# Attention and gated feed-forward on one core: one PSUM bank for queries and keys, one for values and transposed input, two buffers behind them

## What is computed

```python
x = x + layernorm(attention(layernorm(x), W_Q, b_Q, W_K, b_K, W_V, b_V, W_O, b_O))
x = x + layernorm(ffn(layernorm(x), weight, gate_w, lora_U, lora_V))

# attention, 16 heads of 64:
Q, K, V = x W_Q + b_Q, x W_K + b_K, x W_V + b_V
attn = softmax(Q K^T / sqrt(64));  out = (attn V) W_O + b_O
# ffn, 8 experts of rank 16:
gate = softmax(x gate_w^T)
out = x weight^T + sum_e gate_e * (x U_e^T) V_e^T / 16
```

## Time and profile before

| | |
|---|---|
| median of 3 runs | 1090.09 us |
| profiled execution | 1091.16 us |
| its span, first to last instruction | 1089.3 us |
| PE busy | 1021.8 us (94%) |
| DVE busy | 905.9 us (83%) |
| ACT busy | 917.7 us (84%) |
| POOL busy | 800.1 us (73%) |
| mean granted TensorE clock | 0.979 of full speed |

### The profile page before, as it was taken

One profiled execution on the slowest core, in us unless ns is written; L12 is line 12 of the kernel. 1 busy time (PEld: TensorE's weight loads), 2 busy tenths in 40 slices (PEclk: granted clock), 3 DMA queues, 4 the chain that ended last, 5 costly groups with the idle time before them and its releaser, 6 DMA issues.

```text
span 1089.3 us, 28626 instructions
## 1 busy us (share of the span) xinstructions
PE 1021.8 (94%) x8550; PEld 780.2 (72%) x8550; DVE 905.9 (83%) x1630; ACT 917.7 (84%) x3207; POOL 800.1 (73%) x778
## 2 busy tenths in 40 slices
PE   8889999999999999999999999999999999999974
PEld 7767777777777777677777777777767777777743
DVE  6888888888888888888888888888888888888841
ACT  4888888889888888888888989888988888898932
POOL 3676777787777788777778777778877777877741
PEclk9899999999999999999999999999999999999977
DMA  7364566556556556556655655755655665565570
GB/s 239 85 149 108 133 152 144 121 130 142 122 136 159 127 121 146 125 122 153 147 122 125 146 121 132 159 131 122 142 129 121 149 152 122 121 149 123 128 164 11
DMA packets 59219, 145.21 MB, mean 133 GB/s; under 512 B 17216, under 2 KB 25920, under 8 KB 59200
## 3 DMA queue, kind: packets, MB, share of 16 engines
q1 hardware_dynamic: 59200, 144.99, 57.7%
HBM read 6.50 MB, written 4.19 MB: 10 GB/s over the span
## 4 chain that ended last, share of the span: by engine, by line
PE 87%; ACT 4%; issue 3%; DVE 3%; POOL 2%; ACTq 0%; POOLq 0%; DVEq 0%
PE o_ps L460 22%; PE st_ps L438 18%; PE extra_ps L476 8%; PE qk_ps L404 8%; PE qk_ps L406 5%; PE qk_ps L405 5%; PE extra_ps L334 5%; PE extra_ps L418 4%; PE extra_ps L420 3%; PE extra_ps L419 3%; PE extra_ps L497 2%; PE extra_ps L510 2%; ACT v_sb L739 2%; ACT xt_hi L705 1%; PE extra_ps L512 1%
## 5 line engine op out<-in xcount | busy, mean ns | idle before, releaser
L1516 POOL TENSOR_TENSOR probs<-probs,inv_sum 128x1024 f32<-128x1024 f32 x256 | 486.3, 1900 | 201.4 <-DVE inv_sum L1097 201.2
L724 ACT ACTIVATE probs<-st_ps,neg_max 128x256 f32<-128x256 f32 x1024 | 477.9, 483 | 32.5 <-DVE neg_max L1089 30.2
L1089 DVE TENSOR_REDUCE neg_max<-st_ps 128x4 f32<-128x1024 f32 x256 | 310.0, 1211 | 44.7 <-PE st_ps L438 35.5
L1105 DVE STREAM_TRANSPOSE probs_b<-probs 128x1024 f32<-128x1024 f32 x256 | 313.4, 1225 | 26.8 <-POOL probs L1516 26.8
L460 PE MATMUL o_ps<-probs_t,v_sb 128*64 128x256 f32 x2048 | 253.7, 390 | 7.7 <-DVE o_lo L1113 4.3
L724 ACT ACTIVATION_READ_ACCUMULATOR probs<-st_ps,neg_max 128x1 f32 x1024 | 217.9, 213 | 0.0
L460 PEld LDWEIGHTS o_ps<-probs_t,v_sb 128*64 128x64 f32 x2048 | 136.8, 138 | 89.4 <-issue 16.0
L710 ACT CAST qk_hi<-qk_ps 128x512 fp32r<-128x512 f32 x256 | 153.5, 599 | 29.7 <-PE qk_ps L406 26.1
L438 PE MATMUL st_ps<-qk_hi 64*128 64x256 f32 x1024 | 171.9, 332 | 3.8 <-POOL qk_lo L1510 1.5
L438 PE MATMUL st_ps<-qk_lo,qk_hi 64*128 64x256 f32 x1024 | 145.2, 280 | 0.0
L1510 POOL TENSOR_TENSOR qk_lo<-qk_full,qk_hi 128x512 fp32r<-128x512 f32 x96 | 123.5, 1286 | 28.1 <-ACT qk_hi L710 14.6
(11 more groups left out here) (132 smaller groups left out, 1988.6 us busy)
## 6 DMA issues: line engine op xcount, KB each, us to landing
probs_t<-probs_b SPq DMA_DIRECT2D x1024, 128.0 KB, 2.4
out<-x_all SPq DMA_DIRECT2D x31, 128.0 KB, 1.9
x_all<-in_x SPq DMA_DIRECT2D x1, 3840.0 KB, 17.3
probs_b<-in_w_v SPq DMA_DIRECT2D x1, 512.0 KB, 4.9
probs_b<-in_w_o SPq DMA_DIRECT2D x1, 512.0 KB, 6.8
probs_b<-in_w_q SPq DMA_DIRECT2D x1, 384.0 KB, 5.3
probs_b<-in_w_k SPq DMA_DIRECT2D x1, 384.0 KB, 5.9
x_all<-in_x SPq DMA_DIRECT2D x2, 128.0 KB, 3.5
```

The lines of the kernel that those rows point to most:

```text
L724: last = nc.scalar.activation(probs[n][:, h, j, :], st_ps[p % 2][:, (2 * h + j) * T:(2 * h + j + 1) * T], ACT.Exp, bias=neg_max[n][:, h, j ...
L1089: nc.vector.tensor_reduce(neg_max[p % N_PROBS][:, :, :].rearrange("p h j -> p (h j)"), st_ps[p % 2][:, :].rearrange("p (j s) -> p j s", j= ...
L1105: nc.vector.transpose(probs_b[chunk % 2][:, :, :, 2 * NT * n:2 * NT * (n + 1), :].rearrange("p i t n q -> p n t i q"), probs[p % N_PROBS][ ...
L1516: nc.gpsimd.tensor_tensor(probs[n][:, :, :, :].rearrange("p h j s -> p (h j) s"), probs[n][:, :, :, :].rearrange("p h j s -> p (h j) s"), ...
```

## The change

Banks: `qk_ps` becomes one bank, used by every pair in turn, and `project_qk(b, p)` waits until the bank of pair `p - 1` has been read. The bank that this frees, `xv_ps`, holds the transposed input and the value quarters; `extra_ps` keeps the output projection and the feed-forward part. Buffers: `xt_hi`, `xt_lo` and `v_sb` are there twice, and batch `b` uses number `b % 2`. `qk_full` is one buffer for all pairs, and `POOL_LO` has two pairs instead of three, so DVE makes the remainders of six pairs of a batch, not five. To make room in SBUF, `x1t`, `ut` and the squares share the buffers `yt` and `u`, with the waits that this asks for. Loops: a turn holds two batches, with the buffer number as a constant. The order of every engine is written anew: `probs_v` is now two batches behind the projections (before: one), the feed-forward part three (before: two), and `project_qk(b, 4)` to `(b, 7)` and `scores(b, 3)` to `(b, 7)` stand in the body of the next batch.

```diff
-POOL_LO = (1, 4, 6,)
+POOL_LO = (1, 5,)
...
-        xt_hi = sb("xt_hi", [P, T], F32R)
-        xt_lo = sb("xt_lo", [P, T], F32R)
+        xt_hi = [sb(f"xt_hi{n}", [P, T], F32R) for n in range(2)]
+        xt_lo = [sb(f"xt_lo{n}", [P, T], F32R) for n in range(2)]
-        qk_full_sb = {p: sb(f"qk_full{p}", [P, 2 * T]) for p in POOL_LO}
-        v_sb = sb("v_sb", [P, NT, H * DH])
+        qk_full_sb = sb("qk_full", [P, 2 * T])
+        v_sb = [sb(f"v_sb{n}", [P, NT, H * DH]) for n in range(2)]
...
-        qk_ps = [bank(f"qk_ps{n}") for n in range(2)]
+        qk_ps = bank("qk_ps")
+        xv_ps = bank("xv_ps")
...
-            with engine.Fori(0, high - low) as step:
-                body(step + low)
+            with engine.Fori(0, (high - low) // 2) as step:
+                for n in range(2):
+                    body(2 * step + (low + n), (low + n) % 2)
...
-                if (p - 2) % PAIRS in POOL_LO:
-                    after(pe, qk_hi_ready, PAIRS * b + p - 1)
-                after(pe, *qk_bank_read(b, p - 2))
+                if (p - 1) % PAIRS in POOL_LO:
+                    after(pe, qk_hi_ready, PAIRS * b + p)
+                after(pe, *qk_bank_read(b, p - 1))
```

The PE body, of which the diff shows the beginning and the end of the new one; between them stand the projections, scores and `probs_v` that the prediction lists:

```diff
-            def body(i):
+            def body(i, r):
                 transpose_xn(i, free=(v_copied[3], i))
-                scores(i - 1, 7)
-                project_qk(i, 0)
-                project_qk(i, 1)
-                output_projection(i - 2, free=(xt_lo_ready, i + 1))
+                project_qk(i - 1, 4, 1 - r)
+                output_projection(i - 3, free=(z_copied, i - 3))
+                project_qk(i - 1, 5, 1 - r)
+                scores(i - 1, 3)
+                scores(i - 1, 4)
+                project_qk(i - 1, 6, 1 - r)
...
-                scores(i, 6)
-                project_v(i, 3, free=(v_copied[2], i + 1))
+                project_qk(i, 3, r)
+                project_v(i, 3, r, free=(v_copied[2], i + 1))
+                scores(i, 1)
+                scores(i, 2)
...
-            run(pe, 3, B, body)
+            run(pe, 4, B, body)
```

More of the change, by code:

```diff
@@ L386, in transpose_xn, with project_qk @@
                 pe.wait_ge(xn_ready, b + 1)
-                transpose_tiles(extra_ps, xn).then_inc(x_transposed, 1)
-            def project_qk(b, p):
+                transpose_tiles(xv_ps, xn).then_inc(x_transposed, 1)
+            def project_qk(b, p, turn):
                 if first(b) and p == 0:
@@ L416, in project_v @@
                 cols = slice(half * HALF, (half + 1) * HALF)
[L417 to L420, removed]
+                dst = xv_ps[:, :]
+                nc.tensor.matmul(dst, tile(xt_hi[turn], j), w_hi["v"][:, cols], start=True, stop=False)
+                nc.tensor.matmul(dst, tile(xt_hi[turn], j), w_lo["v"][:, cols], start=False, stop=False)
+                nc.tensor.matmul(dst, tile(xt_lo[turn], j), w_hi["v"][:, cols], start=False,
                                  stop=True).then_inc(v_projected[quarter], 1)
@@ new lines, in _ @@
+            probs_v(1, 0, 1)
+            probs_v(1, 1, 1)
+            project_qk(2, 5, 0)
+            project_v(2, 3, 0, free=(v_copied[2], 3))
+            scores(2, 4)
+            transpose_x1(0, free=(x1_ready, 1))
+            project_qk(2, 6, 0)
+            probs_v(1, 2, 1)
+            scores(2, 5)
+            transpose_xn(3, free=(v_copied[3], 3))
+            project_qk(2, 7, 0)
+            probs_v(1, 3, 1)
+            project_tg(0, free=(x1t_ready, 1))
+            project_v(3, 0, 1, free=(xt_lo_ready, 4))
@@ new lines, in _ @@
+            project_qk(3, 0, 1)
+            scores(2, 6)
+            scores(2, 7)
+            probs_v(1, 4, 1)
+            probs_v(1, 5, 1)
+            transpose_u(0, free=(u_ready, 1))
+            project_v(3, 1, 1, free=(v_copied[0], 4))
+            project_qk(3, 1, 1)
+            scores(3, 0)
+            project_v(3, 2, 1, free=(v_copied[1], 4))
+            project_qk(3, 2, 1)
+            probs_v(1, 6, 1)
+            probs_v(1, 7, 1)
+            project_z(0, free=(ut_ready, 1))
@@ new lines, in _ @@
+            probs_v(30, 2, 0)
+            probs_v(30, 3, 0)
+            transpose_x1(29, free=(x1_ready, 30))
+            project_qk(31, 7, 1)
+            scores(31, 6)
+            scores(31, 7)
+            project_tg(29, free=(x1t_ready, 30))
+            probs_v(30, 4, 0)
+            probs_v(30, 5, 0)
+            probs_v(30, 6, 0)
+            probs_v(30, 7, 0)
+            transpose_u(29, free=(u_ready, 30))
+            project_z(29, free=(ut_ready, 30))
+            output_projection(30, free=(z_copied, 30))
@@ new lines, in _ @@
+            run(act, 4, B, body)
+            qk_hi(31, 4)
+            exponentials(31, 1, 0)
+            exponentials(31, 1, 1)
+            exponentials(31, 2, 1)
+            copy_yt(29)
+            exponentials(31, 2, 0)
+            qk_hi(31, 5)
+            square_y(29)
+            qk_full(31, 5)
+            exponentials(31, 3, 0)
+            exponentials(31, 3, 1)
+            attention_hi(30, 0)
+            qk_hi(31, 6)
+            exponentials(31, 4, 1)
+            exponentials(31, 4, 0)
```

1057 lines of the change are left out of this document (598 added, 459 removed).

## The result

The changed kernel takes 998.72 us (median of 4 runs, 998.15 to 999.0) against 1090.13 of the kernel before beside it: a ratio of 0.916, 95% interval 0.9144 to 0.9176. The direction was as forecast, and so was what happens in the loop; the size was not: 1031 was forecast, 1012 to 1062 as the range, and the gain is 91 us instead of 59.

The account below looks back on a forecast made before the run. PE's own instructions plus two gaps were taken to bound the loop. 29 turns x (32.13 - 30.1) = 58.9 us, with 0 for prologue and epilogue, off 1091.16 gave 1032.3 profiled, 1031 as median; range 1012 to 1062.

Parts of the forecast that it names:

- PE is the bound, with two gaps: Loop: PE's own instructions bound it, plus waits for value copy and transposed input, 1.19 us a turn, which go.
- 0.20 us for a change of shape, 22 to 17 of them: PE's loop: each entry into work using the array in another shape costs 0.20 us; five fewer a turn, 1.0 us.
- PE's list of 29.5 us: Loop: PE's calls in the new order, priced one by one, sum to 29.5 us a turn if PE never waits.
- The eight hand-overs fit: Single projection bank in the loop: ACT and DVE read it before each next projection, four times with half a microsecond or less.
- I take 0.65 us of PE waiting a turn: Loop: allowance for missed hand-overs, between 0.1 and 3.5 us, bringing the turn to 30.1 us.
- DVE 28.4 us a turn: Loop: one more subtraction of 0.6 us raises DVE's busy time from 27.8 to 28.4 us of 29.5.
- that rival: Loop: DVE becomes the bound, 2.6 us of its idle time stay, turn 31.0 us, time 1057; chance 0.19.
- Prologue and epilogue: -4 to +4, I take 0: Outside the loop: work of one batch moves there, some may fill the epilogue's 21.8 us of idle PE; net 0 us.
- Loop of two batches: 0: Loop borders: branches cost nothing before, so halving their number gives 0.
- 0.04 for 35 us: Loop start: rival that the longer PE loop is fetched anew, 2.5 us 14 times, 35 us, time 1066; chance 0.04.
- The POOL pair to DVE: hidden in the loop: Loop: one pair's subtraction moves from POOL to DVE, 0.6 us more there, still within the turn.
- Slower by the single bank, 0.08: Ahead of every projection: rival that late hand-overs stall PE 3.5 us a turn, turn 33.0, time 1115; chance 0.08.

Follow-up runs that it names:

- experiment 2: Changed kernel with the last value quarter put right ahead of the transpose again, and ACT's copy of it moved later: 1026.22 us, ratio 0.9426.
- Experiment 3: Changed kernel, six DVE subtractions one long instruction later: 1199.99 us; pair 3's alone one row maximum later: 1026.65; 1.15 us of independent DVE work ahead of pair 3's: 1011.23.
- experiment 4: Changed kernel with unused statistics instructions spread over DVE's turn: five, 1000.58 us (ratio 0.9184); ten, 1017.41 us (0.9344).
- Experiment 5: Extra matmuls in idle PE gaps: kernel before, prologue 1087.46 us, epilogue 1085.72; changed kernel's last batch 996.53, then with and without on one chip 998.24 and 998.17.

## Why the prediction was too high

The profiled execution took 999.0 us where the sum gave 1032.3: 33.3 us, 17.1 of them in the loop (29 times 30.1 - 29.51) and 16.1 outside. Two terms of the sum failed: the waiting that was charged in the loop, and the nothing that was put for prologue and epilogue.

- **PE is the bound, with two gaps: right.** Both gaps went, and experiment 2 brings the first back. It costs 1.01 us a turn there, not only the 0.76 that the list of waits shows. The 2.62 us of a turn are 1.19 of waits, about 0.9 for five changes of shape (0.17 to 0.20 each), 0.25 lost beside the first gap, and 0.3 whose place was not measured, perhaps the same beside the second.
- **0.20 us for a change of shape, 22 to 17 of them: right.** 0.17 to 0.18 measured.
- **PE's list of 29.5 us: right**, 29.51.
- **The eight hand-overs fit: right.** Experiment 3 shows that the price of a miss was put too low: I counted 1.15 us of delay less the room for each, 3.5 us for all eight; one subtraction behind a row maximum costs 1.08 us a turn although its room was 0.6, and six cost 8.0.
- **"I take 0.65 us of PE waiting a turn": the step that failed in the loop.** It measured 0.01. The allowance had no row behind it: I had worked out that every room suffices, and then added a charge for being tight. The durations repeat from turn to turn (29.49 to 29.53 us from the third turn on), so nothing is missed by chance; in experiment 4 DVE is busy for 98% and a turn grows by 0.1 us only. The lower end of that term (0.1) was the value that my own walk had given.
- **DVE 28.4 us a turn: right**, 28.26 (791.16 us in 28 turns). Of its 1.25 us of idle time nearly all could be used, so that rival had no ground.
- **"Prologue and epilogue: -4 to +4, I take 0": the second step that failed**, with -16.1, outside its bounds. I set the batch that moves out against a batch in the loop, took the epilogue's 21.8 us of idle PE for a bound of 4 us only, and did not use the clock of the old prologue (0.92) and epilogue (0.70), which stands in the earlier trace rows. From the clocks, 0.08 x 107.9 x 2 + 0.30 x 49.6 x 2 = 47 us of the old kernel ran at 1.2 GHz and 12 of the new one (0.10 x 61.5 x 2). What the stretches show directly is that the batch of 29.5 us added 19.0 us of busy time, 10.5 less than its own, and filled 5.6 us of idle time; together these are the 16.1. That the 10.5 us of busy time were saved by the clock is argued, not shown. How much a higher clock is worth in time is uncertain: of 19 executions of the kernel before on one chip, those with a mean clock of 0.985 took 1085.6 to 1085.9, those with 0.978 or 0.979 1089.9 to 1091.1, which is 4.5 us for 14 us less at 1.2 GHz, or about 11 for the 35 (an estimate, and from a correlation). Experiment 5 gives less: 3.4 us in the old epilogue, nothing clear in the old prologue, none in the new epilogue.
- **Loop of two batches: 0. Right in the result, for a reason that the prediction did not have.** The doubled ACT loop is fetched anew or not by where it begins; the changed kernel's happens to begin at a good place, which is luck. The prediction looked at PE's loop for this, and it was ACT's. No row of the profile before tells good from bad starts, and its remark that 0.23 MB is less than 29 times any body rests on no row either; 0.04 for 35 us was too little, as three of the five starts tried cost 45 to 50.
- **The POOL pair to DVE: hidden in the loop, right.**
- **Slower by the single bank, 0.08.** It did not happen, but the mechanism is real: with six subtractions one instruction later the kernel is 10% slower than before. The written order is what avoids it.

## What to carry to other kernels

When a walk through the in-order engines shows that every hand-over fits, believe it, and keep the charge for misses in the range, not in the value; then make sure that nothing which itself waits for the bottleneck stands ahead of the step that frees its buffer. Price work that moves between loop and edges by the idle time and the granted clock of the edges; here a batch of 29.5 us cost 13.4 there. And when a loop body grows, look at the packets of the instruction queues: one that is fetched anew may cost half the gain, and some padding ahead of the loop may give it back.

## What the hardware showed that was not expected

- ACT's loop of 284 instructions is fetched anew each turn or not, by where it begins: 321, 450 and 453 bad (80 to 82 packets, 45 to 50 us), 358 and 486 good (15 to 17 packets). PE's loop of 1142 instructions showed no such stall at the starts that it had in these runs (13 or 14 packets in q8).
- DVE can be busy for 98% of a loop in an exchange with four other engines, at a price of 0.2% (587.83 of 600 us); 2% come when its own work of a turn (29.8 us) is longer than PE's.
- PE at 1.2 GHz for a while outside the loop costs less than the half that a busy PE would lose: an estimate of 0.3 us for each microsecond of it from 19 executions of one kernel, and down to nothing measurable where its idle gaps were filled.
